# Splitting the edge weights ahead of the first spans of pairs, with ScalarE copying and GpSimd subtracting

## The reference

```python
def _gcn_conv(x, edge_index, edge_weight, W, b):
    ...
    deg = jax.ops.segment_sum(w, col, num_segments=n)
    dinv = jnp.where(deg > 0, jax.lax.rsqrt(jnp.where(deg > 0, deg, 1.0)), 0.0)
    norm = dinv[row] * w * dinv[col]
...
h = jnp.maximum(_layernorm(x, axis=-1), 0.0)
x = x + _L0_gnn_ref(h, edge_index)
h = jnp.maximum(_layernorm(x, axis=-1), 0.0)
x = x + _L1_gnn_ref(h, edge_index, edge_weight, L1_gnn_W, L1_gnn_b)
```

## Time and profile before

| | |
|---|---|
| three runs | median 1091.03 us (1090.18 to 1092.83) |
| the profiled execution | 1091.64 us, its span 1089.8 us |
| busy share of the span | TensorE 86%, VectorE 77%, ScalarE 41%, GpSimd 52% |
| chain that ended last, by engine | PE 34%, POOL 21%, DVE 20%, issue 12%, ACT 5% |
| instructions | 24033 |

### The profile page before, as it was taken

The page is one execution under the profiler, slowest core; times in us unless marked ns, Lnnn a source line. Parts: engine busy times, 40 slices in busy tenths (PEclk is TensorE's granted clock), DMA queues, the critical chain, the costliest instruction groups (busy, mean ns, idle before and its releaser), DMA issues.

```text
span 1089.8 us, 24033 instructions
## 1 busy us (share of the span) xinstructions
PE 933.4 (86%) x6195; PEld 592.5 (54%) x6195; DVE 835.1 (77%) x2627; ACT 451.3 (41%) x879; POOL 571.7 (52%) x747
## 2 busy tenths in 40 slices
PE   2788888799958878888679969999999999999995
PEld 2465655354536656676454654556555565555553
DVE  8988888743579778889974686777877877777776
ACT  2577777310105545445311234444434444434441
POOL 6534333000016777777600047777777777777770
PEclk9687777799989899989878959999999999999997
DMA  3000000600002111111125055455444544444441
GB/s 65 2 1 0 0 0 0 262 34 1 1 0 49 27 26 27 27 25 27 25 77 190 21 165 116 106 107 105 107 104 102 106 107 100 104 103 101 105 94 33
DMA packets 144600, 72.30 MB, mean 66 GB/s; under 512 B 111661, under 2 KB 136442, under 8 KB 144410
## 3 DMA queue, kind: packets, MB, share of 16 engines
q1 hardware_dynamic: 127224, 54.98, 19.3%
q0 software_dynamic: 15936, 16.35, 8.5%
q10 hardware_dynamic: 1378, 0.22, 0.1%
HBM read 59.13 MB, written 12.35 MB: 66 GB/s over the span
## 4 chain that ended last, share of the span: by engine, by line
PE 34%; POOL 21%; DVE 20%; issue 12%; ACT 5%; DMA 4%; DVEq 2%; ACTq 1%; POOLq 0%; SPq 0%
POOL A L1208 14%; PE seg L1606 12%; POOL pair L1208 7%; ACT A L1343 5%; PE big L1530 4%; PE seg L1733 4%; DVE A L1894 3%; PE big L1769 3%; DMA A<-table,src_i 3%; PE big L1759 2%; PE seg L1780 2%; PE seg L1801 1%; DVE acc_mem L1905 1%; PE seg L1544 1%; DVE A L1883 1%
## 5 line engine op out<-in xcount | busy, mean ns | idle before, releaser
L1208 POOL DMA_INDIRECT A<-table,src_i x338 | 323.1, 956 | 116.8 <-issue 98.6
L1208 POOL DMA_INDIRECT pair<-table,src_i x160 | 160.4, 1003 | 62.6 <-issue 48.5
L1343 ACT CAST A<-big 128x500 f32 x208 | 125.4, 603 | 48.0 <-PE big L1535 24.9
L1733 PE MATMUL seg<-A 128*128 128x384 f16 (+1 forms) x624 | 120.1, 336 | 11.1 <-DVE A L1960 8.2
L1769 PE MATMUL big<-A 128*128 128x512 f32 x208 | 109.9, 610 | 1.5 <-DMA A<-pr_table 1.5
L1636 PE MATMUL big<-A 128*128 128x300 bf16 (+1 forms) x512 | 96.5, 335 | 16.8 <-DVE A L1883 14.6
L1444 ACT COPY A<-big 128x512 f32<-128x512 f32 x104 | 60.8, 584 | 119.8 <-PE big L1759 118.6
L1450 ACT ACTIVATE A<-big,A 128x512 f32<-128x512 f32 x104 | 71.5, 688 | 93.3 <-PE big L1770 92.9
L1733 PEld LDWEIGHTS seg<-A 128*128 128x128 f16 x624 | 57.0, 98 | 89.7 <-issue 36.0
L1606 PE MATMUL seg<-A,acc_mem 128*128 128x512 f16 (+1 forms) x406 | 84.1, 362 | 7.6 <-DVEq L2124 7.6
L1271 POOL COPY cur<-pair 128x24 bf16 x100 | 39.7, 440 | 95.4 <-PE seg L1544 95.4
(11 more groups left out here) (306 smaller groups left out, 1780.3 us busy)
## 6 DMA issues: line engine op xcount, KB each, us to landing
A<-in_edge_attr_dram SPq DMA_DIRECT2D x103, 128.0 KB
A<-drel_flat SPq DMA_DIRECT2D x104, 126.0 KB
spilled_adjacency<-A SPq DMA_DIRECT2D x1, 7074.0 KB, 21.6
A<-spilled_adjacency SPq DMA_DIRECT2D x6, 1152.0 KB, 12.4
A<-table,src_i POOLq DMA_INDIRECT x338
A<-pr_table SPq DMA_DIRECT2D x104, 31.5 KB
pair<-table,src_i POOLq DMA_INDIRECT x160
A<-low_flat SPq DMA_DIRECT2D x78, 32.0 KB
```

Of the source, the lines that this page charges most:

```text
L1208: pool.indirect_dma_start(out=row, out_offset=None, in_=table, in_offset=bass.IndirectOffsetOnAxis(ap=src_i[:, tile:tile + 1], axis=0)).th ...
L1343: nc.scalar.copy(A[:, :, bass.ds(bases[k], PW)], big[:, k % 4, 0:PC].rearrange("p (s d) -> p s d", d=PW)).then_inc(window_kept, 1)
L1733: op = nc.tensor.matmul(made[:, 0:held.shape[2] * D], hot_low[:, u, m, :], held[:, k, :, :], start=(m == 0 and k == 0), stop=(m == 3 and k ...
```

## The change

The split leaves its place behind the clearing of A. Its three roundings go to ScalarE, its two subtractions stay on GpSimd, and both now stand ahead of the mean subtraction (GpSimd) and around the copies that ScalarE makes in the set-up. So that the weights are there by then, TensorE turns the raw weights first of all blocks, and ScalarE copies them out before its second row copy; the counts in the waits for cols_ps go up by one. The pool_link waits go, new signals are w_rounded (ScalarE to GpSimd) and w_left (GpSimd to ScalarE). GpSimd waits for the third rounding ahead of iota_d, and ScalarE's wait for w_parts_ready at the end of the loop of spans is gone. In the numbered lines, L1250 to L1254 of before disappear.

```diff
             pool.memset(w_parts[:, 0:T, 0], 1.0)
+            pool.wait_ge(ev("w_rounded"), 1)
+            pool.tensor_tensor(w_res, wcol[:, 0:T], w_parts[:, 0:T, 1], ALU.subtract).then_inc(ev("w_left"), 1)
+            pool.wait_ge(ev("w_left"), 1)
+            pool.wait_ge(ev("w_rounded"), 2)
+            pool.tensor_tensor(w_res, w_res, w_parts[:, 0:T, 2], ALU.subtract).then_inc(ev("w_left"), 1)
             pool.wait_ge(ev("mean0_ready"), 1)
...
-            pool.wait_ge(ev("edge_cols"), 2)
-            pool_link(pool.tensor_copy(w_parts[:, 0:T, 1], wcol[:, 0:T]))
-            pool_link(pool.tensor_tensor(w_res, wcol[:, 0:T], w_parts[:, 0:T, 1], ALU.subtract))
-            pool_link(pool.tensor_copy(w_parts[:, 0:T, 2], w_res))
-            pool_link(pool.tensor_tensor(w_res, w_res, w_parts[:, 0:T, 2], ALU.subtract))
-            pool_link(pool.tensor_copy(w_parts[:, 0:T, 3], w_res))
-            pool.sem_inc(ev("w_parts_ready"), 1)
+            pool.wait_ge(ev("w_rounded"), 3)
             pool.wait_ge(ev("ranges_ready"), 1)
...
             nc.scalar.copy(src_t, raw_src).then_inc(ev("src_t_ready"), 1)
+            act.wait_ge(ev("cols_ps"), 1)
+            nc.scalar.copy(wcol[:, :], banks[6][:, 0:TK]).then_inc(ev("edge_cols"), 1)
+            act.wait_ge(ev("edge_cols"), 1)
+            nc.scalar.copy(w_parts[:, 0:T, 1], wcol[:, 0:T]).then_inc(ev("w_rounded"), 1)
             act.wait_ge(ev("src_low_ready"), 1)
             nc.scalar.copy(low_16, src_low).then_inc(ev("rows_16_ready"), 1)
-            for n, b, t in ((5, 4, drel[:, :]), (6, 6, wcol[:, :])):
-                act.wait_ge(ev("cols_ps"), n)
-                nc.scalar.copy(t, banks[b][:, 0:TK]).then_inc(ev("edge_cols"), 1)
+            act.wait_ge(ev("w_left"), 1)
+            nc.scalar.copy(w_parts[:, 0:T, 2], w_res).then_inc(ev("w_rounded"), 1)
+            act.wait_ge(ev("cols_ps"), 6)
+            nc.scalar.copy(drel[:, :], banks[4][:, 0:TK]).then_inc(ev("edge_cols"), 1)
+            act.wait_ge(ev("w_left"), 2)
+            nc.scalar.copy(w_parts[:, 0:T, 3], w_res).then_inc(ev("w_rounded"), 1)
...
-            act.wait_ge(ev("w_parts_ready"), 1)
             nc.scalar.copy(src_i[:, :], banks[5][:, 0:TK]).then_inc(ev("src_kept"), 1)
...
+            pe.wait_ge(ld_edges, 13 * 16)
+            for c in range(4):
+                op = nc.tensor.transpose(banks[6][:, c * P:(c + 1) * P], raw_w[:, c * P:(c + 1) * P], ident[:, :])
+            op.then_inc(ev("cols_ps"), 1)
             turn_rows0(0, dst_t, "dst_t")
...
             turn_rows0(4, drel_t, "drel_t")
-            for c in range(4):
-                op = nc.tensor.transpose(banks[6][:, c * P:(c + 1) * P], raw_w[:, c * P:(c + 1) * P], ident[:, :])
-            op.then_inc(ev("cols_ps"), 1)
...
-            dve.wait_ge(ev("cols_ps"), 4)
+            dve.wait_ge(ev("cols_ps"), 5)
```

## The result

The changed kernel takes 1084.24 us (median of 6 runs, 1083.36 to 1088.04) against 1090.76 of before (6 runs, 1088.60 to 1092.83): 6.5 us less, a ratio of 0.9940 with a 95% interval of 0.9924 to 0.9956. A second set, on the chip of the first experiments, gave 1085.02 against 1090.73, 0.9948 (0.9937 to 0.9960). The forecast was 1088.1 us, and its range ended at 1086.3. The profiled execution is 1083.36 us with a span of 1081.6, where before had 1091.64 and 1089.8.

The account below looks back on a forecast made before the run. VectorE, held by GpSimd's split, was taken to bound the first span. 3.8 us gained there less 0.9 paid ahead made 2.9 us, so the median of 1091.03 becomes 1088.1 us; 8-in-10 range 1086.3 to 1090.2.

Parts of the forecast that it names:

- What bounds the first span: First span: VectorE alone bounds it, its hot_r held by GpSimd's split instructions, 4.50 us against 1.77 for the same work.
- hot_r is held by some other cause: First span: hot_r stays at 1058 ns with GpSimd idle, nothing gained, front costs 0.9, 1091.9 us; chance 0.03.
- TensorE becomes the bound of this span: First span: windows stay 1.19 us apart, total gain 1.8 us; chance 0.16 together with the front that costs twice.
- wider hot_r are not held: First span: hot_r of 400 columns took 224 ns, read as not held; those of 300 took 1058 ns, read as held.
- The gain there: First span: without the split VectorE's hot_r end at 29.06 instead of 32.85, 3.8 us earlier.
- TensorE's and ScalarE's cover: First span: TensorE's windows every 0.63 us leave VectorE 0.56 us to spare; ScalarE's eighth copy ends near 32.2, before 33.6.
- The price ahead of the spans: Ahead of the mean subtraction: the first GpSimd subtraction holds VectorE's short instructions, delaying the chain by 0.9 us.
- the free front, my first rival: Ahead of the spans: the first subtraction slips under the reduction, costing 0.4 us; gain 3.4, 1087.6 us; chance 0.2.
- The second: Ahead of the spans: the second GpSimd subtraction runs beside the feature reduction, cost taken as 0, open up to 1.09 us.
- the first part: Section on what bounds the kernel now; it took the loop from span 1, 6.43 us a span, as unchanged.
- The sum: Whole kernel: 3.8 us gained in the first span less 0.9 paid ahead of the spans, 2.9 us.
- My third rival: Loop of spans: loses to TensorE's clock, at worst all 24 spans at 6.86 us, 1098.4 us; chance 0.04.

Follow-up runs that it names:

- the first experiments: The changed kernel once more, unedited, on one chip with the next three runs: 1085.02 us, ratio 0.9948.
- without subtractions: Changed kernel without its two GpSimd subtractions, all three roundings reading the weight itself (weighted degree wrong): 1083.50 us, ratio 0.9933.
- the extra matmuls: Ten unused 300-column matmuls between span 0 and span 1: 1084.82 us (0.9942) in the changed kernel, 1090.70 us (0.9998) in the one before.

## Why the prediction was wrong

What bounds the first span: right. hot_r was held by GpSimd's instructions, and where they are gone it runs freely (2.23 us instead of 4.50). With that two rivals fall: that hot_r is held by some other cause and the change does nothing, and that TensorE becomes the bound of this span. Wrong was only the reading of the earlier trace rows that wider hot_r are not held.

The gain there: forecast 3.8, measured 3.89 without subtractions. TensorE's and ScalarE's cover held: the windows came 0.63 us apart.

The price ahead of the spans: forecast 0.9, measured 1.05. The first subtraction got in between the four comparisons, as taken, and held one for 0.84; the free front, my first rival, did not come. The second held not the reduction but the small st_c behind it for 0.23, which I had at 0. One duration was outside its bounds: a rounding on ScalarE takes 1.14 us, not 0.45 to 0.61.

```profile
17.02 1.14 ACT L1328 CAST pair<-wcol 128x416 bf16<-128x416 f32 x1
```

It writes every fourth bfloat16, and the rows that I sized it by write side by side. I take the spacing for the cause: a cast of 512 columns from float32 to float16 side by side took 0.62 us on ScalarE in the kernel before (at 14.92 us), but no run parts the spacing from the type bfloat16. That put the first subtraction at 18.24 instead of 17.7 and the second at 20.61 instead of 19.5, so late that it met st_c. The cover on ScalarE was wide enough for the rest.

The step that failed is one sentence of the first part: "I take that loop, and all behind it, as moved along unchanged." The sum was right to 0.1 us at hot_d of span 1 (2.84 against 2.9; there is some luck in it, since 0.09 too little gain and 0.15 too little price nearly cancel) and wrong by 3.9 at the end of the loop. I looked at the three roundings as work that is covered (it is), and not as three instructions ahead of a loop. And I never asked which engine bounds that loop: it is ScalarE, whose way over the jump has no slack, so that 0.15 us of its sequencer comes back 24 times. My third rival had seen that the loop may change its pace, but named TensorE's clock for it and the other sign; the extra matmuls and span 6 at either clock speak against it.

What stays open: what the border in the instruction stream is and when the next one comes, and the last part of the profiled pair's difference. The spans differ by 8.2 us, the last hot_d by 6.8; the rest lies within the scatter of what follows the loop. The medians of the two sets lie 6.5 and 5.7 us apart; the intervals of both hold 2.8 + 3.9 = 6.7.

## What to carry to other kernels

An instruction that nobody waits for yet may still cost most of its length on another engine (here about 0.8 us for each GpSimd subtraction of 1.08), so a step off the chain is best put beside the kind of work that it doesn't hold, here beside reductions. An edit that adds or removes instructions ahead of a loop is also an edit of that loop: look at which engine bounds it, compare its way over the jump before and after, and move the loop by a few cheap instructions alone before the gain is put down to anything else. Size an instruction by a row with the same access pattern, not just the same number of elements.

## What the runs showed of the hardware that was not expected

ScalarE's sequencer took 1.27 to 1.28 us or 1.12 us over the same loop jump, by where the loop lies in its instruction stream; the longer pause moved by one instruction for each instruction put ahead and was gone with three and eight more in the kernel before, and with one more in the changed one. A rounding from float32 to every fourth bfloat16 took 1.14 us for 416 elements on ScalarE, while a cast of 512 side by side took 0.61. A hot_r of 400 columns that met a GpSimd subtraction was held as those of 300 columns were (517 ns in the mean of four, against 311 where GpSimd was idle). And VectorE's st_c, with 25 columns and 0.18 us alone, was held by GpSimd as well (0.41 us).
